# Linear attention of a hybrid block: factor tables by GpSimd beside the statistics, normalised tiles by ScalarE, two constant factors folded into neighbouring operations

## The chip, the cores and the metric

The kernel runs on one core of one Trainium2 chip. The metric is the device time of one execution in microseconds (us), lower is better. All data is fp32; a batch holds 1,024 tokens of 128 channels, and there are 8 batches.

## What is computed

The whole kernel is a chain of a convolutional attention, a whitening, a linear attention, a mixture of experts with GELU, a window attention and a mixture of experts with SiLU. The change touches the linear attention alone. Cut to that:

```python
def _ln_t(v, eps=1e-05):                       # over the 128 channels of a token
    return (v - mean(v)) / sqrt(var(v) + eps)

def _L2_attn_ref(x, kln_weight, kln_bias, vln_weight, vln_bias):
    # 8 heads of 16 channels; k and v are both a layer norm of the head's 16 channels
    q = qkv = x.reshape(B, N, H, hc).transpose(0, 2, 1, 3)
    k = _layernorm(qkv, kln_weight, kln_bias)   # (x - mean) / (std(ddof=1) + 1e-5), then weight and bias
    v = _layernorm(qkv, vln_weight, vln_bias)
    kv = jnp.einsum('bhnd,bhne->bhde', k, v) / N
    out = jnp.einsum('bhnd,bhde->bhne', q, kv)
    return out + x

t = t + _L2_attn_ref(_ln_t(t), ...)
```

## The kernel before, in words

`tokens` is a tensor of 128 partitions x 64 tiles x 128 channels that stays on chip through the program; a batch is 8 of its tiles. `linear_attention` is a block of its own: all engines wait at a barrier before it and after it, so nothing of the stages around it runs beside it. Each engine has its own program, written out by hand, and runs it in that order; semaphores tie the programs together. Most buffers (offset, square, std, scale, z, u, uT, kv) are doubled by the parity of the batch.

- **VectorE** first takes the statistics of all 64 tiles (`TokenNorm.run`, L618 to L650), ending in `norm.mean` and `norm.rstd` (128 x 64). Then it gives `norm_ready` (L770), builds four 128 x 128 tables `factor` (L777 to L781: an outer product of a weight row and a weight column, times a mask of the head blocks), and goes through the batches. One `step(b)` (L839) is: `centre_heads(b+1)` (L791 sum over a head's 16 channels, L792 times 1/16, L793 subtract from the tokens, giving `offset`), `keys(b)` (L811 to L815 on 128 x 64, L816 makes `z`), `variance(b+1)` (L799 sums the squares, L802 times 1/15), `add(b-2)` (L836, twice, adds a result to `tokens`), `combine(b-1)` (L824 to L830, builds the 128 x 128 matrix `kv`). Steps 0, 1 and 7 lack parts of it; steps 2 to 5 stand in a loop, 6 and 7 behind it.
- **ScalarE** per batch: square of `offset(b+1)` (L868), square root (L870) of the variance, and two copies of the transposed tiles, `uT(b)` (L877).
- **GpSimd** makes constants, and then, per batch, the normalised tiles `u` in two operations on 128 x 1024 with broadcast operands (L755, L757); it waits for `norm_ready`, and later for the transposes of two batches before.
- **TensorE** per batch: 8 transposes of `u` (L899, waits for `u` and for `uT` of the batch before), 8 products `z^T z` with a column of ones beside (L903, waits for `z`), 8 column sums (L906), and 8 products of the batch before with `kv` (`give`, L916).
- **SyncE** loads the four small weights at the start (L731, L733).

Of the kernel before, what the change touches and what calls it, by code (L numbers as in the profile page):

```python
# [5 lines left out]
ALU = mybir.AluOpType  # L6
ACT = mybir.ActivationFunctionType
# [662 lines left out]
def linear_attention(nc, ins, ident, tokens):  # L670
# [6 lines left out]
    with ExitStack() as ctx:  # L677
# [11 lines left out]
        var = [t.sbuf(f"lvar{i}", [P, NT * HEADS2]) for i in range(2)]  # L689
# [24 lines left out]
        var_ready = t.sem("lvar_ready")  # L714
        std_ready = t.sem("lstd_ready")
        z_ready = t.sem("z_ready")
        norm_ready = t.sem("lnorm_ready")
        centred = t.sem("lcentred")
# [18 lines left out]
        def _(pool):  # L737
# [11 lines left out]
            def normalise(b, par, first=False):  # L749

                if not first:
                    pool.wait_ge(turn_ready, b - 1)
                at = bass.ds(b * NT, NT)
                over = lambda x: x[:, at].unsqueeze(2).to_broadcast([P, NT, C])
# [12 lines left out]
        def _(dve):  # L767
            norm.run(dve, tokens)

            dve.tensor_copy(term[:, 0:1], norm.rstd[:, 0:1]).then_inc(norm_ready, 1)  # L770
            dve.wait_ge(norm_ready, 1)


            steps = Steps(dve, setup_steps)
            dve.wait_ge(params_loaded, 64)
            dve.wait_ge(blocks_ready, 1)
# [10 lines left out]
            def centre_heads(b, par):  # L787

                centre.round(b)
                batch = tokens[:, bass.ds(b * NT, NT), :].rearrange("p j (h d) -> p (j h) d", h=HEADS2)  # L790
                centre.then(dve.tensor_reduce(head_sum[par][:, :], batch, AX.X, ALU.add))  # L791
                centre.then(dve.tensor_scalar(head_sum[par][:, :], head_sum[par][:, :], 1.0 / HC, None, ALU.mult))  # L792
                dve.tensor_tensor(offset[par][:, :].rearrange("p (g d) -> p g d", d=HC), batch,  # L793
                                  head_sum[par][:, :].unsqueeze(2).to_broadcast([P, NT * HEADS2, HC]),
                                  ALU.subtract).then_inc(offset_ready, 1)

            def variance(b, par):
                dve.wait_ge(square_ready, b + 1)
                dve.tensor_reduce(head_sum[par][:, :], square[par][:, :].rearrange("p (g d) -> p g d", d=HC),  # L799
                                  AX.X, ALU.add).then_inc(squares_summed, 1)  # L800
# [51 lines left out]
            variance(0, 0)  # L852
# [1689 lines left out]
```

## Time and profile before

| | |
|---|---|
| median of 3 runs | 1689.6 us (1680.47 to 1693.16) |
| the profiled execution's own time | 1682.29 us |
| its span, first to last instruction | 1680.4 us |
| mean granted TensorE clock (share of full) | 0.828 |
| busy over the span: PE, DVE, ACT, POOL | 1292.0, 989.6, 519.9, 592.2 us |
| first and last instruction of the linear attention | 297.5 us, 417.7 us |

The span is the time between the first and the last instruction on the chip; the run's time lies 1.9 us above it. PE is TensorE, DVE VectorE, ACT ScalarE, POOL GpSimd. Because of the barriers the linear attention is a stretch of 120 us of its own, and its length adds to the time one for one.

### The profile page before, as it was taken

To read this page: it belongs to the slowest core of one execution; us is meant where nothing else is said; L and a number is where in the kernel's file an instruction comes from. 1 tells how busy PE (TensorE), PEld (TensorE's weight loads), DVE (VectorE), ACT (ScalarE), POOL (GpSimd) and SP (SyncE) were. 2 spreads that over 40 slices of the span, in tenths; PEclk is the share of its full clock that TensorE was granted. 3 is DMA by queue.
4 is the path that set the end of the run, shared out by engine and by line. 5 is a ranking of instruction groups with operands and counts; after the bars stand their busy time and mean duration, and the time that the engine had idled before them with its cause. 6 is when DMAs were issued, how large, how long until landed. Compare 5 with 4: busy or idle time off the path is not lost. (4 is left out here: it accounts for less than half of the span.)

```text
span 1680.4 us, 31908 instructions
## 1 busy us (share of the span) xinstructions
PE 1292.0 (77%) x11786; PEld 1088.7 (65%) x11786; DVE 989.6 (59%) x2376; ACT 519.9 (31%) x1183; POOL 592.2 (35%) x640
## 2 busy tenths in 40 slices
PE   6999987066582999889966775767664999999950
PEld 3555567066572999889953543534453999999950
DVE  3777765898654444455436545643336777788841
ACT  3444420021431545444433221321131233222220
POOL 4000000232145656555025330166103661455554
PEclk9999997589555999999986775666656999999985
DMA  7600000000401333333241200011001332333341
GB/s 278 238 0 1 1 4 0 4 1 0 120 29 61 117 110 115 100 105 111 73 102 41 60 26 1 8 43 42 15 0 55 108 106 85 94 100 105 98 141 50
DMA packets 87890, 115.45 MB, mean 69 GB/s; under 512 B 18695, under 2 KB 70275, under 8 KB 87747
## 3 DMA queue, kind: packets, MB, share of 16 engines
q1 hardware_dynamic: 66786, 62.73, 12.0%
q0 software_dynamic: 20960, 50.76, 9.6%
q8 instruction: 96, 1.57, 0.4%
q14 instruction: 48, 0.39, 0.1%
HBM read 53.01 MB, written 60.42 MB: 68 GB/s over the span
## 5 line engine op out<-in xcount | busy, mean ns | idle before, releaser
L1304 POOL DMA_INDIRECT sorted_rows<-s_normed,s_places x128 | 138.3, 1080 | 222.7 <-POOLq L2404 94.0
L1380 POOL DMA_INDIRECT sx_fetch<-sorted_results,s_places x128 | 132.6, 1036 | 143.1 <-DMA sx_fetch<-sorted_results,s_places 62.1
L1304 POOL DMA_INDIRECT sorted_rows<-g_normed,g_places x128 | 130.2, 1017 | 111.0 <-DMA sorted_rows<-g_normed,g_places 48.7
L1463 PE MATMUL g_bank<-weights,gx_hT 128*128 x1360 | 167.1, 277 | 0.0
L1380 POOL DMA_INDIRECT gx_fetch<-sorted_results,g_places x128 | 125.0, 977 | 114.8 <-DMA gx_fetch<-sorted_results,g_places 64.7
L1463 PEld LDWEIGHTS g_bank<-weights,gx_hT 128*128 128x128 f32 x1360 | 160.1, 193 | 0.2 <-issue 0.2
L1428 PE MATMUL s_bank<-sx_xT_high,sx_w_now 128*128 128x256 f32 (+1 forms) x510 | 151.4, 297 | 1.8 <-DVE sx_hT L1533 1.2
L1430 PE MATMUL s_bank<-sx_xT_high,sx_w_now 128*128 128x256 f32 (+1 forms) x510 | 143.9, 282 | 0.0
L1429 PE MATMUL s_bank<-sx_xT_low,sx_w_now 128*128 128x256 f32 (+1 forms) x510 | 143.8, 282 | 0.0
L1463 PE MATMUL s_bank<-weights,sx_hT 128*128 (+1 forms) x1020 | 130.4, 277 | 7.0 <-issue 4.5
L1488 ACT ACTIVATE gx_hT<-g_bank,gx_b_now 128x256 f32<-128x256 f32 x340 | 133.1, 485 | 3.0 <-PE g_bank L1463 3.0
L1463 PEld LDWEIGHTS s_bank<-weights,sx_hT 128*128 128x128 f32 (+1 forms) x1020 | 120.4, 191 | 12.4 <-issue 12.1
L1428 PE MATMUL g_bank<-gx_xT_high,gx_w_now 128*128 128x256 f32 x340 | 104.6, 308 | 22.9 <-DVE gx_w_now L1516 10.2
L234 PE MATMUL attended<-probs,vs 128*128 128x512 f32 x256 | 120.3, 593 | 0.0
L1481 ACT ACTIVATE sx_xT_high<-s_bank 128x256 fp32r<-128x256 f32 x85 | 32.7, 384 | 241.1 <-PE s_bank L1463 197.2
L339 ACT ACTIVATE probs<-score,nmax 128x1024 f32<-128x1024 f32 x64 | 71.3, 1115 | 113.5 <-DVE nmax L281 113.5
L1542 DVE TENSOR_TENSOR gx_yq<-g_bank,weights 128x256 f32<-128x256 f32 x85 | 36.0, 423 | 119.7 <-PE g_bank L1463 94.7
L281 DVE TENSOR_REDUCE nmax<-score 128x1 f32<-128x1024 f32 x64 | 78.2, 1223 | 46.0 <-PE score L223 46.0
L1429 PE MATMUL g_bank<-gx_xT_low,gx_w_now 128*128 128x256 f32 x340 | 97.6, 287 | 0.0
L1430 PE MATMUL g_bank<-gx_xT_high,gx_w_now 128*128 128x256 f32 x340 | 97.4, 287 | 0.0
L1428 PEld LDWEIGHTS s_bank<-sx_xT_high,sx_w_now 128*128 128x128 f32 (+1 forms) x510 | 90.9, 178 | 2.4 <-issue 2.3
L1481 ACT ACTIVATE gx_xT_high<-g_bank 128x256 fp32r<-128x256 f32 x85 | 32.9, 387 | 188.3 <-PE g_bank L1463 118.5
(404 smaller groups left out, 2920.6 us busy)
## 6 DMA issues: line engine op xcount, KB each, us to landing
sorted_rows<-zeros POOLq DMA_DIRECT2D x29, 512.0 KB, 16.6
gx_xq<-sorted_rows SPq DMA_DIRECT2D x85, 128.0 KB
sorted_results<-gx_yq SPq DMA_DIRECT2D x85, 128.0 KB
sx_xq<-sorted_rows SPq DMA_DIRECT2D x85, 128.0 KB
sorted_results<-sx_yq SPq DMA_DIRECT2D x85, 128.0 KB
feats<-in_x SPq DMA_DIRECT2D x8, 512.0 KB, 4.9
out<-s_normed SPq DMA_DIRECT2D x16, 256.0 KB
g_raw_up<-in_L_ffn_W SPq DMA_DIRECT2D x1, 2048.0 KB, 9.3
```

Of the source, the lines that this page charges most:

```text
L234: done = pe.matmul(out[:, HALF * h:HALF * h + HALF], vs[s % 4][:, :], probs[s % 4][:, HALF * h:HALF * h + HALF], start=(n == 0), stop=(n = ...
L281: dve.tensor_reduce(nmax[s % 4][:, :], score[s % 2][:, :], AX.X, ALU.max, negate=True).then_inc(max_ready, 1)
L339: act.activation(probs[s % 4][:, :], score[s % 2][:, :], ACT.Exp, bias=nmax[s % 4][:, 0:1], accum_out=zsum[s % 4][:, 0:1]).then_inc(exp_do ...
L1304: pool.indirect_dma_start(out=sorted_rows[g], out_offset=bass.IndirectOffsetOnAxis(ap=places[:, at, r:r + 1], axis=0), in_=normed[:, at, : ...
L1380: pool.indirect_dma_start(out=fetch[n % 2][:, i, r, :], out_offset=None, in_=self.sorted_results[g], in_offset=bass.IndirectOffsetOnAxis(a ...
L1428: pe.matmul(out, left[:, part, columns], right[0][:, :], start=True, stop=False)
L1429: pe.matmul(out, left[:, part, columns], right[1][:, :], start=False, stop=False)
L1430: pe.matmul(out, left[:, part + 1, columns], right[0][:, :], start=False, stop=True)
L1463: done = pe.matmul(down[u % 2][:, P * k:P * k + C], hT[u % 2][0:width, i, P * k:P * k + P], self.w_down[0:width, bass.ds(e, 1), i, :].rear ...
L1481: act.activation(xT[u % 2][0][:, :], self.turned[u % 2][:, 0:UNIT], ACT.Copy).then_inc(self.x_high, 1)
L1488: done = act.activation(hT[i][:, k, :], up[i][k // 2][:, k % 2, :], ACT.Gelu, bias=self.b_now[u % 4][:, k:k + 1])
L1542: dve.tensor_tensor(self.yq[u % 4][:, :, :], product, bias, ALU.add).then_inc(self.y_ready, 1)
```

## The change

The four tables `factor` are made on GpSimd right after its constants, as soon as the weights are loaded; VectorE waits for them (`factors_ready`) behind `variance(0)`. `u` is made by ScalarE in 8 instructions of 128 x 128 a batch, `rstd * x + shift`, for which VectorE makes `shift = -mean * rstd` once. The multiplication by 1/16 (L792) goes into the subtraction as a constant of a scalar_tensor_tensor, and that by 1/15 (L802) into the square root's scale.

```diff
-                pool.tensor_tensor(u[par][:, :, :], tokens[:, at, :], over(norm.mean), ALU.subtract).then_inc(centred, 1)
-                pool.wait_ge(centred, b + 1)
-                pool.tensor_tensor(u[par][:, :, :], u[par][:, :, :], over(norm.rstd), ALU.mult).then_inc(u_ready, 1)
...
-            pool.wait_ge(norm_ready, 1)
-            normalise(0, 0, first=True)
-            normalise(1, 1, first=True)
-            with pool.Fori(2, B - 1, 2) as b:
-                normalise(b, 0)
-                normalise(b + 1, 1)
+            factors = Steps(pool, setup_steps)
+            pool.wait_ge(params_loaded, 64)
+            pool.wait_ge(blocks_ready, 1)
+            pairs = ((0, 0, 1.0 / N), (0, 1, 1.0 / N), (1, 0, 1.0 / N), (1, 1, 1.0))
+            for i, (col, row, over) in enumerate(pairs):
+                factors.did(pool.tensor_scalar(factor[i][:, :], rows[:, row, :], column[:, col:col + 1], over,
+                                               ALU.mult, ALU.mult))
+            factors.settle()
+            for i in range(4):
+                factors.did(pool.tensor_tensor(factor[i][:, :], factor[i][:, :], blocks[:, :], ALU.mult))
+            factors.settle()
+            pool.tensor_tensor(factor[3][:, :], factor[3][:, :], ident[:, :], ALU.add).then_inc(factors_ready, 1)
...
-            dve.tensor_copy(term[:, 0:1], norm.rstd[:, 0:1]).then_inc(norm_ready, 1)
-            dve.wait_ge(norm_ready, 1)
-            for i, (col, row, over) in enumerate(((0, 0, 1.0 / N), (0, 1, 1.0 / N), (1, 0, 1.0 / N), (1, 1, 1.0))):
-                steps.then(dve.tensor_scalar(factor[i][:, :], rows[:, row, :], column[:, col:col + 1], over,
-                                             ALU.mult, ALU.mult))
-                steps.then(dve.tensor_tensor(factor[i][:, :], factor[i][:, :], blocks[:, :], ALU.mult))
-            steps.then(dve.tensor_tensor(factor[3][:, :], factor[3][:, :], ident[:, :], ALU.add))
+            dve.scalar_tensor_tensor(out=shift[:, :], in0=norm.mean[:, :], scalar=-1.0, in1=norm.rstd[:, :],
+                                     op0=ALU.mult, op1=ALU.mult).then_inc(norm_ready, 1)
...
                 centre.then(dve.tensor_reduce(head_sum[par][:, :], batch, AX.X, ALU.add))
-                centre.then(dve.tensor_scalar(head_sum[par][:, :], head_sum[par][:, :], 1.0 / HC, None, ALU.mult))
-                dve.tensor_tensor(offset[par][:, :].rearrange("p (g d) -> p g d", d=HC), batch,
-                                  head_sum[par][:, :].unsqueeze(2).to_broadcast([P, NT * HEADS2, HC]),
-                                  ALU.subtract).then_inc(offset_ready, 1)
+                dve.scalar_tensor_tensor(out=offset[par][:, :].rearrange("p (g d) -> p g d", d=HC),
+                                         in0=head_sum[par][:, :].unsqueeze(2).to_broadcast([P, NT * HEADS2, HC]),
+                                         scalar=-1.0 / HC, in1=batch, op0=ALU.mult, op1=ALU.add
+                                         ).then_inc(offset_ready, 1)
...
-                dve.wait_ge(squares_summed, b + 1)
-                dve.tensor_scalar(var[par][:, :], head_sum[par][:, :], 1.0 / (HC - 1), None,
-                                  ALU.mult).then_inc(var_ready, 1)
...
             centre_heads(0, 0)
             variance(0, 0)
+            dve.wait_ge(factors_ready, 1)
...
-                act.wait_ge(var_ready, b + 1)
-                act.activation(std[par][:, :], var[par][:, :], ACT.Sqrt).then_inc(std_ready, 1)
+                act.wait_ge(squares_summed, b + 1)
+                act.activation(std[par][:, :], square_sum[par][:, :], ACT.Sqrt, scale=1.0 / (HC - 1)
+                               ).then_inc(std_ready, 1)
+            def normalise(b, par, first=False):
+                if not first:
+                    act.wait_ge(turn_ready, b - 1)
+                for j in range(NT):
+                    at = bass.ds(b * NT + j, 1)
+                    done = act.activation(u[par][:, j, :], tokens[:, at, :].rearrange("p a c -> p (a c)"), ACT.Identity,
+                                          bias=shift[:, at], scale=norm.rstd[:, at])
+                done.then_inc(u_ready, 1)
...
                 if after:
                     square_of(b + 1, 1 - par)
+                    normalise(b + 1, 1 - par, first=first)
                 act.wait_ge(turn_ready, b + 1)
```

VectorE, between the end of the statistics and the first batches. Before, these rows stood behind the reciprocal that makes `rstd` (the first pair of table rows comes four times in all; `head_sum` is the sum over a head):

```order
L650 RECIPROCAL lnorm_rstd<-lnorm_root 128x64
L770 COPY lterm<-lnorm_rstd 128x1
L778 TENSOR_SCALAR lfactor<-lrows,lcolumn 128x128
L780 TENSOR_TENSOR lfactor<-lfactor,lblocks 128x128
...
L781 TENSOR_TENSOR lfactor<-lfactor,ident 128x128
L791 TENSOR_REDUCE head_sum<-tokens 128x64
L792 TENSOR_SCALAR head_sum<-head_sum 128x64
L793 TENSOR_TENSOR offset<-tokens,head_sum 128x1024
L799 TENSOR_REDUCE head_sum<-square 128x64
L802 TENSOR_SCALAR lvar<-head_sum 128x64
```

Now the same place reads (line numbers of the changed kernel):

```order
L650 RECIPROCAL lnorm_rstd<-lnorm_root 128x64
L766 SCALAR_TENSOR_TENSOR lnorm_shift<-lnorm_mean,lnorm_rstd 128x64
L777 TENSOR_REDUCE head_sum<-tokens 128x64
L778 SCALAR_TENSOR_TENSOR offset<-head_sum,tokens 128x1024
L785 TENSOR_REDUCE lsquare_sum<-square 128x64
```

The nine rows of the tables are gone from VectorE, and so are one row behind each sum over tokens and one behind each sum of squares.

ScalarE, in the first batches. Before (the row on `lnorm_root` is the root of the statistics):

```order
L616 ACTIVATE lnorm_root<-lnorm_eps_var 128x64
L868 ACTIVATE square<-offset 128x1024
L870 ACTIVATE lstd<-lvar 128x64
L868 ACTIVATE square<-offset 128x1024
L870 ACTIVATE lstd<-lvar 128x64
L877 ACTIVATE luT<-lturn 128x512 x2
```

Now:

```order
L616 ACTIVATE lnorm_root<-lnorm_eps_var 128x64
L852 ACTIVATE square<-offset 128x1024
L854 ACTIVATE lstd<-lsquare_sum 128x64
L863 ACTIVATE lu<-tokens,lnorm_shift,lnorm_rstd 128x128 x8
L852 ACTIVATE square<-offset 128x1024
L854 ACTIVATE lstd<-lsquare_sum 128x64
L863 ACTIVATE lu<-tokens,lnorm_shift,lnorm_rstd 128x128 x8
L873 ACTIVATE luT<-lturn 128x512 x2
```

Eight instructions stand between each square root and the copies of the transposed tiles (and, in the first batch, ahead of the second square).

GpSimd, behind its constants. Before, the normalisation stood there, with a loop for batches 2 to 7; now the tables:

```order
L746 AFFINE_SELECT lblocks<-lblocks 128x128
L755 TENSOR_TENSOR lu<-tokens,lnorm_mean 128x1024
L757 TENSOR_TENSOR lu<-lu,lnorm_rstd 128x1024
```

```order
L746 AFFINE_SELECT lblocks<-lblocks 128x128
L754 TENSOR_SCALAR lfactor<-lrows,lcolumn 128x128 x4
L758 TENSOR_TENSOR lfactor<-lfactor,lblocks 128x128 x4
L760 TENSOR_TENSOR lfactor<-lfactor,ident 128x128
```

Sixteen large operations of GpSimd, all behind the statistics, have given way to nine small ones that wait only for the weights.

## Rows read from the trace of the kernel before

**Rows 1.** Stretches: us; PE, PEld, DVE, ACT, POOL busy (count); clock, DMA, GB/s.
```profile
351.80:362.90 11.10, 7.42 (x45) 7.19 (x46) 10.72 (x20) 2.28 (x4) 4.83 (x2) 0.75 0.00 0
395.10:404.40 9.30, 7.49 (x65) 7.06 (x64) 8.92 (x20) 2.28 (x4) 0.00 (x0) 1.00 0.00 0
351.80:404.40 52.60, 37.69 (x280) 35.93 (x280) 50.48 (x92) 11.43 (x20) 18.32 (x8) 0.90 0.00 0
```

**Rows 2.** Timeline where VectorE builds the tables: start us, us, engine, line, operation.
```profile
317.13 0.15 DVE L770 COPY lterm<-lnorm_rstd 128x1 f32<-128x1 f32 x1
...
317.37 1.99 POOL L755 TENSOR_TENSOR lu<-tokens,lnorm_mean 128x1024 f32<-128x1024 f32 x1 [18.65 <-DVE lterm L770]
317.64 1.86 DVE L780 TENSOR_TENSOR lfactor<-lfactor,lblocks 128x128 f32<-128x128 f32 x1
...
329.84 1.22 DVE L791 TENSOR_REDUCE head_sum<-tokens 128x64 f32<-128x1024 f32 x1
```

**Rows 3.** Timeline of step 2, VectorE and GpSimd.
```profile
355.11 1.90 POOL L755 TENSOR_TENSOR lu<-tokens,lnorm_mean 128x1024 f32 x1 [4.32 <-PE lturn L899]
355.54 1.55 DVE L815 TENSOR_TENSOR lscale<-lscale,lnorm_rstd 128x64 f32<-128x64 f32 x1
...
357.17 2.93 POOL L757 TENSOR_TENSOR lu<-lu,lnorm_rstd 128x1024 f32<-128x1024 f32 x1 [0.16 <-POOL lu L755]
...
359.51 0.64 DVE L802 TENSOR_SCALAR lvar<-head_sum 128x64 f32<-128x64 f32 x1
```

**Rows 4.** Groups of instructions, 297 to 418 us: busy us, mean ns, idle before.
```profile
L815 DVE TENSOR_TENSOR lscale<-lscale,lnorm_rstd 128x64 f32<-128x64 f32 x8 | 5.6, 697 | 0.3
...
L826 DVE SCALAR_TENSOR_TENSOR kv<-lfactor,lsums,kv 128x128 f32<-128x128 f32 x8 | 4.6, 578 | 0.3
...
L802 DVE TENSOR_SCALAR lvar<-head_sum 128x64 f32<-128x64 f32 x8 | 4.1, 515 | 0.3
```

**Rows 5.** Timeline of step 6, with no GpSimd work beside it, VectorE.
```profile
395.11 1.21 DVE L791 TENSOR_REDUCE head_sum<-tokens 128x64 f32<-128x1024 f32 x1
...
396.36 0.20 DVE L792 TENSOR_SCALAR head_sum<-head_sum 128x64 f32<-128x64 f32 x1
...
396.58 1.23 DVE L793 TENSOR_TENSOR offset<-tokens,head_sum 128x1024 f32<-128x1024 f32 x1
...
400.20 1.21 DVE L799 TENSOR_REDUCE head_sum<-square 128x64 f32<-128x1024 f32 x1
...
401.44 0.20 DVE L802 TENSOR_SCALAR lvar<-head_sum 128x64 f32<-128x64 f32 x1
401.55 1.28 DVE L836 TENSOR_TENSOR tokens<-tokens,lresult 128x512 f32<-128x512 f32 x2
...
403.13 0.35 DVE L826 SCALAR_TENSOR_TENSOR kv<-lfactor,lsums,kv 128x128 f32<-128x128 f32 x1
...
404.38 0.22 DVE L811 TENSOR_TENSOR lscale<-lstd,lnorm_rstd 128x64 f32<-128x64 f32 x1
```

**Rows 6.** ScalarE's operations, by line: duration ns min/median/max, first and last start.
```profile
L868 ACT ACTIVATE square<-offset x8: 1056/1056/1058, 332.6 to 397.8; 128x1024 f32<-128x1024 f32 x8
...
L877 ACT ACTIVATE luT<-lturn x16: 578/588/597, 341.8 to 408.0; 128x512 f32<-128x512 f32 x16
```

**Rows 7.** Timeline of a later stage: eight of L1147 in a row.
```profile
428.66 3.19 ACT L1147 ACTIVATE g_normed<-tokens,gr_norm_shift,gr_norm_rstd 128x128 f32<-128x128 f32 x8 [0.87 <-DVE gr_norm_shift L1034]
```

**Rows 8.** The weights' last load: its issue, and us to landing in the DMA view.
```profile
298.80 0.43 SPq L733 DMA_DIRECT2D lrows<-in_L_attn_vln_bias  x1
...
lrows<-in_L_attn_vln_bias SPq DMA_DIRECT2D x1, 64.0 KB, 4.2
```

**Rows 9.** GpSimd's nearest small operation, by line, whole program.
```profile
L746 POOL TENSOR_SCALAR_AFFINE_SELECT lblocks<-lblocks 128x128 f32<-128x128 f32 x1 | 0.3, 337 | 0.1
```

**Rows 10.** Timeline: first products of the stage, and its last row.
```profile
340.26 3.71 PE L903 MATMUL gram<-z 128*128 128x129 f32 x16 [16.84 <-DVE z L816]
...
416.40 1.28 DVE L836 TENSOR_TENSOR tokens<-tokens,lresult 128x512 f32<-128x512 f32 x2 [2.21 <-PE lresult L916]
```

More of the change, by code:

```diff
@@ L688, in linear_attention @@
         norm = TokenNorm(t, "l")
-        var = [t.sbuf(f"lvar{i}", [P, NT * HEADS2]) for i in range(2)]
+        shift = t.sbuf("lnorm_shift", [P, TT])
+        square_sum = [t.sbuf(f"lsquare_sum{i}", [P, NT * HEADS2]) for i in range(2)]
         std = [t.sbuf(f"lstd{i}", [P, NT * HEADS2]) for i in range(2)]
@@ L713, in linear_attention @@
         square_ready = t.sem("square_ready")
-        var_ready = t.sem("lvar_ready")
         std_ready = t.sem("lstd_ready")
         z_ready = t.sem("z_ready")
+        factors_ready = t.sem("lfactors_ready")
         norm_ready = t.sem("lnorm_ready")
-        centred = t.sem("lcentred")
         u_ready = t.sem("lu_ready")
@@ L747, in _ @@
                                pattern=[[HC, HEADS2], [0, HC]], channel_multiplier=-1).then_inc(blocks_ready, 1)
[L749 to L754, printed above, removed]
-                pool.tensor_tensor(u[par][:, :, :], tokens[:, at, :], over(norm.mean), ALU.subtract).then_inc(centred, 1)
-                pool.wait_ge(centred, b + 1)
-                pool.tensor_tensor(u[par][:, :, :], u[par][:, :, :], over(norm.rstd), ALU.mult).then_inc(u_ready, 1)
-            pool.wait_ge(norm_ready, 1)
-            normalise(0, 0, first=True)
-            normalise(1, 1, first=True)
-            with pool.Fori(2, B - 1, 2) as b:
-                normalise(b, 0)
-                normalise(b + 1, 1)
+            factors = Steps(pool, setup_steps)
[10 more added lines that the diff above has]
+            pool.tensor_tensor(factor[3][:, :], factor[3][:, :], ident[:, :], ALU.add).then_inc(factors_ready, 1)
         @block.vector
@@ L791, in centre_heads @@
                 centre.then(dve.tensor_reduce(head_sum[par][:, :], batch, AX.X, ALU.add))
-                centre.then(dve.tensor_scalar(head_sum[par][:, :], head_sum[par][:, :], 1.0 / HC, None, ALU.mult))
-                dve.tensor_tensor(offset[par][:, :].rearrange("p (g d) -> p g d", d=HC), batch,
-                                  head_sum[par][:, :].unsqueeze(2).to_broadcast([P, NT * HEADS2, HC]),
-                                  ALU.subtract).then_inc(offset_ready, 1)
+                dve.scalar_tensor_tensor(out=offset[par][:, :].rearrange("p (g d) -> p g d", d=HC),
+                                         in0=head_sum[par][:, :].unsqueeze(2).to_broadcast([P, NT * HEADS2, HC]),
+                                         scalar=-1.0 / HC, in1=batch, op0=ALU.mult, op1=ALU.add
+                                         ).then_inc(offset_ready, 1)
             def variance(b, par):
                 dve.wait_ge(square_ready, b + 1)
-                dve.tensor_reduce(head_sum[par][:, :], square[par][:, :].rearrange("p (g d) -> p g d", d=HC),
+                dve.tensor_reduce(square_sum[par][:, :], square[par][:, :].rearrange("p (g d) -> p g d", d=HC),
                                   AX.X, ALU.add).then_inc(squares_summed, 1)
-                dve.wait_ge(squares_summed, b + 1)
-                dve.tensor_scalar(var[par][:, :], head_sum[par][:, :], 1.0 / (HC - 1), None,
-                                  ALU.mult).then_inc(var_ready, 1)
             def keys(b, par):
@@ L868, in square_of, with batch @@
                 act.activation(square[par][:, :], offset[par][:, :], ACT.Square).then_inc(square_ready, 1)
-                act.wait_ge(var_ready, b + 1)
-                act.activation(std[par][:, :], var[par][:, :], ACT.Sqrt).then_inc(std_ready, 1)
-            def batch(b, par, after=True):
+                act.wait_ge(squares_summed, b + 1)
[9 more added lines that the diff above has]
+                done.then_inc(u_ready, 1)
+            def batch(b, par, after=True, first=False):
                 if after:
                     square_of(b + 1, 1 - par)
+                    normalise(b + 1, 1 - par, first=first)
                 act.wait_ge(turn_ready, b + 1)
@@ L880, in _ @@
             norm.root_of(act)
+            act.wait_ge(norm_ready, 1)
             square_of(0, 0)
-            batch(0, 0)
+            normalise(0, 0, first=True)
+            batch(0, 0, first=True)
             batch(1, 1)
```

3 lines of the change are left out of this document (removed).

## The prediction

> **What bounds the kernel now.** The stage that changes stands between two barriers, so only its own length counts: it runs from 297.5 us to the end of its last row, 416.40 + 1.28 = 417.7 us [rows 10]. The view of busy time by stretch says which engine sets it: over the five steps from 351.8 to 404.4 us VectorE is busy for 50.5 of 52.6 us, TensorE for 37.7, ScalarE for 11.4, GpSimd for 18.3 [rows 1]. VectorE is the bound, and what counts is its queue. Then the timeline, read for operations that take longer than they should. Step 6, where GpSimd has nothing left to do, goes from 395.11 to 404.38, 9.27 us [rows 5]; the four steps ahead of it share the other 52.6 - 9.3 = 43.3 us, 10.8 each [rows 1, 5], with the same instructions. The difference is in small operations beside GpSimd: L815, on 128 x 64 elements, takes 1.55 us and ends at 357.09, where GpSimd's L755 (355.11 to 357.01) has just ended; GpSimd's next one takes 2.93 us instead of 1.90, and L802 starts under it and ends (360.15) as it does (360.10) [rows 3]. The tables at the start show it strongest: L780, on 128 x 128 elements, takes 1.86 us beside L755, more than L793's 1.23 on eight times as many [rows 2, 5]. And all of the tables lie on the path: from 317.13 us to 329.84 us VectorE does nothing for the batches [rows 2].
>
> **The change, part by part.**
>
> *The tables leave VectorE.* Before, `norm_ready` is given by the copy at 317.13 and the first sum over tokens starts at 329.84 [rows 2]. Now one scalar_tensor_tensor on 128 x 64 stands between, of a size with L811's 0.22 us [rows 5]; the sum does not depend on it and starts about 0.15 us after it does: at 317.3. Gain: 329.84 - 317.3 = **12.5 us**. The cover is GpSimd: the last load is issued at 298.80 and lands 4.2 us later, 303.0 [rows 8]. Nine operations on 128 x 128 follow. Their nearest row from below is 0.34 us (one input, same size) [rows 9], from above 1.90 us (two inputs, eight times the elements) [rows 3]. At 0.34 they end at 306.1, at 1.90 at 320.1; I take 0.35 to 0.4, being the same size. VectorE asks for them behind `variance(0)`, at about 322 us (next part), so even the upper bound is hidden; beyond it each us is lost one for one. They now run beside the statistics; should each hold VectorE up for its own length, that costs 9 x 0.35 = 3.2 us, which I keep for the range.
>
> *Two multiplications go.* L792 to L793 is 0.22 us from start to start, L802 to L836 0.11 [rows 5], and both come once per batch: 8 x 0.22 + 8 x 0.11 = **2.6 us**. The subtraction becomes a scalar_tensor_tensor; the trace has that form only on small tiles (L826, 0.35 us undisturbed on 128 x 128 [rows 5]), where the instruction's fixed part weighs most. On 128 x 1024 I take 1.23 us as L793 [rows 5]; 0.1 more on each of eight would cost 0.8. The constant in the square root costs nothing.
>
> *GpSimd's sixteen operations go.* What they did to VectorE stands in the mean durations: L815 0.697 us against 0.23 undisturbed, L826 0.578 against 0.35, L802 0.515 against 0.20 [rows 4, 5]; times eight, 3.7 + 1.8 + 2.5 = **8.0 us**. Cross-check: four steps at 10.8 instead of 9.27 are 6.2 us, the rest lies in step 1. The Trainium skill (SBUF — State Buffer, "Practical consequences" under the ports) says that a VectorE instruction with two SBUF inputs, or in a two-port mode, and a GpSimd one that reads SBUF exclude each other for a whole instruction, and that tensor_reduce never contends. By that rule the whole 8.0 us comes back; if the stretches had another cause, such as the loop, none of it would. The trace bears the rule out: L799 keeps 1.21 us, L815 does not.
>
> *ScalarE takes the normalisation.* Eight of the same form take 3.19 us in a row [rows 7]. Its other four (square, root, two copies) are 2.28 us per step [rows 1], of which the square is 1.06 and the copies, overlapping, the most of the rest [rows 6]. What matters is its cycle: square root, normalise, copies of `uT`, next square, VectorE's sum of squares: 2.28 + 3.19 + 1.21 = 6.7 [rows 1, 5, 7], with handoffs about 7.1 us. VectorE's step is 9.27 - 0.22 - 0.11 = 8.94. ScalarE has 1.8 us of room per step, and one normalising instruction could cost (8.94 - 7.1 + 3.19)/8 = 0.63 us instead of 0.40 before it bounds. In the loop each gets its addresses from registers; VectorE's do too there and keep their durations, so I take 0.40.
>
> The first batches have less room. Walk: sum at 317.3, offset done 319.8, square 320.9, sum of squares until 322.1, step 0 begins at 322.1. It has neither `add` nor `combine`: 401.55 - 395.11 - 0.33 = 6.1 us [rows 5], so step 1 begins at 328.2. In it ScalarE does root (328.5), normalise(1) (331.7), `uT(0)` (332.8), square(2) (333.8); VectorE asks for the square 4.9 us into its step (400.20 - 395.11 - 0.22 [rows 5]), at 333.1. It waits **0.8 us**. What is late next is the square root of batch 2, whose cycle then has the full step of 8.94. No second wait.
>
> *TensorE* keeps its instructions. It is busy 7.5 us per step at full clock [rows 1], so with 8.94 us it has 1.4 us in hand, and results are used one and two steps later. The tail (from 404.38 to 417.7) waits for TensorE's products, whose inputs move with it; it keeps its 13.3 us.
>
> Sum: 12.5 + 2.6 + 8.0 - 0.8 = **22.3 us**. Against the profiled execution's 1682.3 that is 1660.0; that execution is 7.3 us faster than the median of the runs shown (1689.6, spread 12.7). I predict for the median: 1689.6 - 22.3 = **1667 us**, a gain of 1.3%.
>
> The Trainium skill (GPSIMD Engine Reference, "Engine selection") advises VectorE for elementwise work, as GpSimd is about twice as slow with two inputs. By it nine operations at twice VectorE's 0.35 us [rows 5] are an estimated 6.3 us, ending at 309.3 instead of 306.5: the rule speaks against the move where GpSimd is waited for, and changes nothing in the sum here. No row before shows GpSimd on these shapes.
>
> **The rivals.**
>
> *Half the gain.* The stretches inside the steps stay (contention is not their cause, or ScalarE's many small instructions make a new wait of a us per step). Gain 22.3 - 8.0 = 14.3: 1675 us. For it: step 2 to 5 stand in a loop and step 6 does not, so loop and contention coincide there. Against: both ends of the stretches match GpSimd's ends within 0.1 us [rows 3], and L780 at 317.64 is stretched outside any loop [rows 2]. Chance 0.14.
>
> *ScalarE becomes the bound.* Above 0.63 us per normalising instruction. At 1.0 us its cycle is 3.9 + 8 = 11.9 us, 3.0 over VectorE's, seven times: 21 us, nearly all of the gain: 1688. It would take two and a half times the pace of [rows 7]. Chance 0.04.
>
> *TensorE becomes the bound, and the kernel slower.* The granted clock is 0.75 in step 2, 0.90 over the five steps, 1.00 in step 6, and half, 1.2 GHz, at the stage's first products, which take 3.71 us for sixteen after an idle time of 17 us [rows 1, 10]. At 1.2 GHz throughout a batch takes 2 x 7.5 = 15 us; eight from 327 us (340.26 less 13) end at 447, 29 later than now: 1719. It costs something from a mean clock of 7.5/8.94 = 0.84 downwards (TensorE's share at full clock), and eats the gain at 7.5 x 8/(417.7 - 327) = 0.66. Against: 0.90 was granted at a duty of 7.5 in 10.5 us, and the duty now rises to 7.5 in 8.94. Chance 0.05. A clock between 0.75 and 0.84 costs up to 1 us per step and is in the range.
>
> *Tables late.* Over 2.1 us each, more than eight times the elements take. Chance 0.02.
>
> **The numbers.** Forecast 0.73, half 0.14, the others 0.11, something unlooked for 0.02. Range: below, no stall, `shift` for nothing and the low end of the runs' spread give 1655; above, the half gain with 3 to 5 us of contention or clock gives 1680. What one can tell from no change here is about 1%, 17 us; the forecast is 5 us beyond it, and the half gain and some of the forecast's spread fall inside. Faster 0.70, same 0.25, slower 0.05.
>
> **What would show it.** In the profile of the changed kernel: first sum over tokens at about 317.3; nine table rows on GpSimd ending before 310, with VectorE's statistics rows unchanged; L794 to L799 (before L811 to L816) undisturbed; steps of 8.9 us; one wait for a square of about 0.8 us in step 1; eight normalising rows in 3.2 us; last row of the stage at 395. It is wrong if ScalarE's rows in the loop are spaced by over 0.6 us, if VectorE waits for `square` or for TensorE in every step, or if the tables are waited for.

## The result, and the profile after

| | before | changed |
|---|---|---|
| median of 4 runs | 1691.4 us (1680.5 to 1693.6) | 1662.4 us (1659.9 to 1667.8) |
| profiled execution | 1682.3 us | 1660.95 us |
| span of it | 1680.4 us | 1659.0 us |

The ratio is 0.9876, with a 95% interval of 0.9832 to 0.9920: faster by 1.24%, a small gain, but the interval ends below 1. The forecast was 1667 us in a range of 1655 to 1680, with 0.70 on faster.

Runs of one kernel differ by several us, up to 13 us in the kernel before, so the study reads the stage alone: from the issue of its first load to the end of its last addition to `tokens`, both in the trace. It is 417.68 - 297.48 = 120.2 us before (its end in [rows 10]) and 392.04 + 1.28 - 295.77 = 97.55 us after, 22.65 us less; the two profiled executions differ by 21.3 us in all.

The timeline of the changed kernel, the last load's issue by SyncE (SPq) and VectorE, GpSimd and ScalarE between the loads and the second batch (start us, us, engine, line, operation, idle before and its releaser):

```profile
297.09 0.43 SPq L733 DMA_DIRECT2D lrows<-in_L_attn_vln_bias  x1
300.40 1.43 POOL L754 TENSOR_SCALAR lfactor<-lrows,lcolumn 128x128 f32<-128x128 f32 x4 [3.38 <-DMA lrows<-in_L_attn_vln_bias]
300.67 3.88 DVE L621 BATCH_NORM_STATS2 lnorm_bn<-tokens  x16 [0.40 <-issue]
301.92 1.69 POOL L758 TENSOR_TENSOR lfactor<-lfactor,lblocks 128x128 f32<-128x128 f32 x4
303.69 0.45 POOL L760 TENSOR_TENSOR lfactor<-lfactor,ident 128x128 f32<-128x128 f32 x1
...
315.44 0.22 DVE L766 SCALAR_TENSOR_TENSOR lnorm_shift<-lnorm_mean,lnorm_rstd 128x64 f32<-128x64 f32 x1
315.59 1.21 DVE L777 TENSOR_REDUCE head_sum<-tokens 128x64 f32<-128x1024 f32 x1
316.83 1.22 DVE L778 SCALAR_TENSOR_TENSOR offset<-head_sum,tokens 128x1024 f32<-128x1024 f32 x1
...
320.66 3.17 ACT L863 ACTIVATE lu<-tokens,lnorm_shift,lnorm_rstd 128x128 f32<-128x128 f32 x8
```

It answers to [rows 2, 8]. The tables are done at 304.1 us, 16 us ahead of step 0, which asks for them at 320.4, and VectorE's statistics take 3.88 us for sixteen beside them, against 3.86 us in rounds with GpSimd idle. The sum over tokens follows `shift` by 0.15 us. The offset, now a scalar_tensor_tensor, still takes 1.22 us, as in [rows 5].

Two stretches of the same timeline, the wait in step 1 and a step of the loop, VectorE:

```profile
331.76 1.22 DVE L785 TENSOR_REDUCE lsquare_sum<-square 128x64 f32<-128x1024 f32 x1 [0.46 <-ACT square L852]
...
361.21 1.21 DVE L777 TENSOR_REDUCE head_sum<-tokens 128x64 f32 x1
362.46 1.23 DVE L778 SCALAR_TENSOR_TENSOR offset<-head_sum,tokens 128x1024 f32<-128x1024 f32 x1
...
364.67 0.22 DVE L798 TENSOR_TENSOR lscale<-lscale,lnorm_rstd 128x64 f32<-128x64 f32 x1
364.93 1.22 DVE L799 TENSOR_TENSOR z<-offset,lscale 128x1024 f32<-128x1024 f32 x1
366.07 1.21 DVE L785 TENSOR_REDUCE lsquare_sum<-square 128x64 f32<-128x1024 f32 x1
367.20 1.27 DVE L819 TENSOR_TENSOR tokens<-tokens,lresult 128x512 f32 x2
...
370.02 1.21 DVE L777 TENSOR_REDUCE head_sum<-tokens 128x64 f32<-128x1024 f32 x1
```

A step is 370.02 - 361.21 = 8.81 us; the four steps of the loop take 8.8 to 9.0, from 334.55 to 370.02, where the kernel before took 43.3 us for them. L798 and L809, which answer to L815 and L826 in [rows 3, 4], are back at their bare length, in the loop as well. The groups of the changed kernel (busy us, mean ns, idle before):

```profile
L809 DVE SCALAR_TENSOR_TENSOR kv<-lfactor,lsums,kv 128x128 f32<-128x128 f32 x8 | 2.8, 352 | 0.3
...
L798 DVE TENSOR_TENSOR lscale<-lscale,lnorm_rstd 128x64 f32<-128x64 f32 x8 | 1.8, 225 | 0.3
```

TensorE costs something at the end. Here are two stretches of the changed kernel in the columns of [rows 1] (clock third from the end), then TensorE's slow products and VectorE's addition that waits behind them:

```profile
335.00:370.00 35.00, 28.87 (x230) 27.24 (x228) 33.64 (x64) 22.36 (x51) 0.00 (x0) 0.95 0.00 1
374.00:382.00 8.00, 6.98 (x48) 6.98 (x48) 7.11 (x15) 4.30 (x11) 0.00 (x0) 0.79 0.00 0
```
```profile
377.57 2.92 PE L904 MATMUL gram<-z,lones 128*128 128x128 f32 x16
...
382.31 1.28 DVE L819 TENSOR_TENSOR tokens<-tokens,lresult 128x512 f32<-128x512 f32 x2 [0.93 <-PE lresult L914]
```

The stage in three pieces, from the trace:

| us | before | changed | difference | forecast |
|---|---|---|---|---|
| first load to first sum over tokens | 32.36 | 19.82 | -12.54 | -12.5 |
| from there to the keys of step 7 | 74.54 | 63.24 | -11.30 | -9.8 |
| from there to the end | 13.30 | 14.49 | +1.19 | 0 |
| stage | 120.20 | 97.55 | -22.65 | -22.3 |

### The profile page after: what moved, and what is told of

The parts are those of the page before. It is cut to its first block and busy times, and to the rows that moved or that the text cites. A ratio compares the mean times of both kernels' runs of the same rounds, so it can differ in the third digit from the quotient of the medians.

```text
span 1659.0 us, 31967 instructions
## 1 busy us (share of the span) xinstructions
PE 1281.8 (77%) x11786; PEld 1084.3 (65%) x11786; DVE 966.3 (58%) x2351; ACT 545.0 (33%) x1247; POOL 563.6 (34%) x633
## 3 DMA queue, kind: packets, MB, share of 16 engines
q1 hardware_dynamic: 66786, 62.73, 12.2%
## 5 line engine op out<-in xcount | busy, mean ns | idle before, releaser
L1378 POOL DMA_INDIRECT sx_fetch<-sorted_results,s_places x128 | 136.0, 1062 | 149.1 <-DMA sx_fetch<-sorted_results,s_places 60.7
```

The costliest lines, as they stand in the source:

```text
L1378: pool.indirect_dma_start(out=fetch[n % 2][:, i, r, :], out_offset=None, in_=self.sorted_results[g], in_offset=bass.IndirectOffsetOnAxis(a ...
```

## The experiments

Ten kernels were run, in three groups. Where a ratio is given it is to the kernel before, in the same group of runs. e4, e5, e6, e8, e9 and e10 were run once each, so for them only the stage in the trace is read. Two of its three pieces say how well that repeats: the first took 19.80 to 19.82 us in all nine kernels that build the tables on GpSimd, and the last 13.30 to 13.31 us or, where TensorE's clock is low at its start, 14.49 us (changed, e1, e9); only in e6 is it another, 16.06. An operation is called held when it takes longer than its bare length, its shortest time, because it waits for GpSimd; the hold is the difference.

### The tables back on VectorE (e1)

```diff
-            factors = Steps(pool, setup_steps)
...
+            dve.wait_ge(norm_ready, 1)
+            steps = Steps(dve, setup_steps)
...
+                steps.then(dve.tensor_scalar(factor[i][:, :], rows[:, row, :], column[:, col:col + 1], over,
+                                             ALU.mult, ALU.mult))
+                steps.then(dve.tensor_tensor(factor[i][:, :], factor[i][:, :], blocks[:, :], ALU.mult))
+            steps.then(dve.tensor_tensor(factor[3][:, :], factor[3][:, :], ident[:, :], ALU.add))
```

> The change, but with the four tables built by VectorE again, where they stood before; GpSimd makes only its constants and has nothing to do beside VectorE. Stage length is counted from the first load's issue to the end of the last addition: 120.2 us in the kernel before, 97.6 in the changed one. Theory (the 12.5 us of the tables were mostly waits for GpSimd's large operations, L780 1.86 us): nine operations at about 0.3 us each, stage 97.6 + 2.9 = 100.5 us, table rows of 0.29 us. Rival (the tables cost what they cost, wherever GpSimd is): stage 97.6 + 12.5 = 110 us.

Stage 396.32 - 295.69 = 100.6 us, ratio 0.9899 (0.9835 to 0.9964). The timeline of this run at the tables:

```profile
315.60 0.29 DVE L762 TENSOR_SCALAR lfactor<-lrows,lcolumn 128x128 f32<-128x128 f32 x1
315.92 0.29 DVE L764 TENSOR_TENSOR lfactor<-lfactor,lblocks 128x128 f32<-128x128 f32 x1
...
318.19 0.29 DVE L765 TENSOR_TENSOR lfactor<-lfactor,ident 128x128 f32<-128x128 f32 x1
```

All nine take 0.29 us, 2.9 us from the first to the sum over tokens behind them. The theory holds and the rival falls: of the 12.5 us only a quarter was the tables' own work; the rest was GpSimd's normalisation running beside them.

### GpSimd normalises, the rest changed (e2)

GpSimd's part of the kernel before stands again, behind the tables; ScalarE's is taken out.

```diff
+            pool.wait_ge(norm_ready, 1)
+            normalise(0, 0, first=True)
+            normalise(1, 1, first=True)
...
-                    normalise(b + 1, 1 - par, first=first)
```

> The change, but u is normalised by GpSimd in two operations of 128 x 1024 per batch as before, and not by ScalarE; the tables stay on GpSimd ahead of it and the two constants stay folded. Theory (contention between GpSimd and VectorE made the 8 us in the steps): the steps with GpSimd work take about 10.2 to 10.5 us instead of 8.9, and the first four GpSimd operations (7.6 us), which before ran beside the tables, now run beside batches 0 and 1 and hold VectorE there for 0 to 4 us: stage 105.5 to 110 us. Rival (the steps became shorter for another reason, such as the two operations fewer): stage 97 to 99 us.

Stage 408.40 - 298.63 = 109.8 us, ratio 0.9924 (0.9877 to 0.9970), at the upper end of the expected 105.5 to 110. Its timeline shows where the gain of the moved tables went:

```profile
318.61 1.90 POOL L769 TENSOR_TENSOR lu<-tokens,lnorm_mean 128x1024 f32<-128x1024 f32 x1 [11.69 <-DVE lnorm_shift L784]
319.69 1.89 DVE L796 SCALAR_TENSOR_TENSOR offset<-head_sum,tokens 128x1024 f32<-128x1024 f32 x1
320.58 2.76 POOL L771 TENSOR_TENSOR lu<-lu,lnorm_rstd 128x1024 f32<-128x1024 f32 x1
...
326.29 1.92 DVE L812 TENSOR_TENSOR lscale<-lstd,lnorm_rstd 128x64 f32<-128x64 f32 x1
328.09 1.89 POOL L769 TENSOR_TENSOR lu<-tokens,lnorm_mean 128x1024 f32 x1
328.24 1.79 DVE L814 TENSOR_SCALAR lscale<-lscale 128x64 f32<-128x64 f32 x1
```

The same GpSimd operations now hold the offset and the scales of the first batches instead of the tables. There are six of them (batches 0 to 2), here as beside the tables of the kernel before, not the four that the expectation counts. The piece up to the first sum is 12.5 us shorter than in e3 below (19.81 for 32.35), the piece behind it 6.5 us longer (76.66 for 70.13).

### The two folded constants alone (e3)

```diff
-                centre.then(dve.tensor_scalar(head_sum[par][:, :], head_sum[par][:, :], 1.0 / HC, None, ALU.mult))
...
+                dve.scalar_tensor_tensor(out=offset[par][:, :].rearrange("p (g d) -> p g d", d=HC),
...
-                dve.tensor_scalar(var[par][:, :], head_sum[par][:, :], 1.0 / (HC - 1), None,
-                                  ALU.mult).then_inc(var_ready, 1)
...
+                act.activation(std[par][:, :], var[par][:, :], ACT.Sqrt, scale=1.0 / (HC - 1)).then_inc(std_ready, 1)
```

> The kernel before with the two constants folded and nothing else. Theory (prediction's step): 8 x 0.22 + 8 x 0.11 = 2.6 us less, stage 117.6 us. Second possibility within the contention theory: L802 was where VectorE was held, for 2.5 us in sum, and the row behind it has only one input in SBUF and is not held, so that goes too: stage 115 us. Rival (the hold moves to another row): stage 118 to 120 us.

Stage 413.16 - 297.37 = 115.8 us, 4.4 less, ratio 0.9957 (0.9925 to 0.9988). That lies between the two expected values. Holds moved as well as vanished: in the groups of this run L812 is held less than L815 was in [rows 4] (0.697), L823 more than L826 was (0.578), and L826, whose bare length is 0.29 us, is held as well:

```profile
L823 DVE SCALAR_TENSOR_TENSOR kv<-lfactor,lsums,kv 128x128 f32<-128x128 f32 x8 | 6.0, 751 | 0.3
...
L812 DVE TENSOR_TENSOR lscale<-lscale,lnorm_rstd 128x64 f32<-128x64 f32 x8 | 4.6, 576 | 0.3
...
L826 DVE TENSOR_TENSOR kv<-kv,lterm 128x128 f32<-128x128 f32 x8 | 3.7, 467 | 0.3
```

The two folds are worth 3.6 us where nothing is held (8 x 0.45, worked out under the two multiplications below), and L802 takes its hold of 2.5 us with it; of that, about 1.7 us came back on other rows. So the rival's mechanism, the hold that moves, is there too, in part.

With these three runs there is a small table of the stage, all with the constants folded:

| us | GpSimd normalises | ScalarE normalises | difference |
|---|---|---|---|
| tables on VectorE | 115.8 (e3) | 100.6 (e1) | 15.2 |
| tables on GpSimd | 109.8 (e2) | 97.55 (changed) | 12.2 |
| difference | 6.0 | 3.1 | |

The normalisation's move is worth 12 to 15 us, the tables' 3 to 6, and their gains overlap. Both kernels in which ScalarE normalises have the last piece of 14.49 us, the other two 13.30, so without that clock the normalisation's share would be 1.2 us more.

### Unused GpSimd work beside the changed kernel (e4, e8, e9, e10, e5)

All five add two GpSimd operations per batch, on tiles nobody reads, at the places of the old normalisation; what differs is their form. e4:

```diff
+                if not first:
+                    pool.wait_ge(turn_ready, b - 1)
+                for k in range(2):
+                    pool.tensor_tensor(idle[k][:, :], idle[2][:, :], idle[3][:, :], ALU.mult).then_inc(besides, 1)
+                pool.wait_ge(besides, 2 * b + 2)
```

> The changed kernel, with sixteen additional GpSimd operations of 128 x 1024 with two inputs, on tiles of their own that nobody uses, at the places where the normalisation stood before (two per batch, behind the same waits). Theory (contention): VectorE's small operations are stretched again, L798, L809 and those beside, steps of 10.2 to 10.5 us, stage 105.5 to 110 us, as with GpSimd normalising. Rival (the dependence on u mattered, not the port): stage 97.6 us.

Stage 416.74 - 298.80 = 117.9 us. The rival falls: no batch needs this work, and the stage is 20.4 us longer. But it is 8 us more than expected. Two things plainly differ from the old normalisation: no wait stands between the two, and both operands are full, which makes them longer: 2.35 us instead of 1.90.

e8 has the wait (the second reads what the first wrote):

```diff
+                pool.tensor_tensor(idle[par][:, :], idle[2][:, :], idle[3][:, :], ALU.mult).then_inc(besides, 1)
+                pool.wait_ge(besides, 2 * b + 1)
+                pool.tensor_tensor(idle[par][:, :], idle[par][:, :], idle[3][:, :], ALU.mult).then_inc(besides, 1)
```

> As the run with reading GpSimd operations beside (stage 117.9 us, where the two of a batch stood back to back and z was held for 2.0 us on average), but the second reads what the first wrote and waits for it, as the normalisation did. Theory (the wait leaves a gap of 0.16 us in which a waiting VectorE operation gets in, and then GpSimd waits for it): z back to 1.23 us, GpSimd's second operation at 2.9 us in some batches, stage 108 to 111 us, as with GpSimd normalising (109.8). Rival (the gap makes no difference): 117 to 119 us.

Stage 416.36 - 297.02 = 119.3 us: the time is the rival's. Its timeline shows the race for `z`:

```profile
350.20 2.34 POOL L773 TENSOR_TENSOR idle<-idle 128x1024 f32<-128x1024 f32 x1 [3.63 <-PE lturn L919]
350.44 2.18 DVE L820 TENSOR_TENSOR lscale<-lscale,lnorm_rstd 128x64 f32<-128x64 f32 x1
352.62 2.34 POOL L775 TENSOR_TENSOR idle<-idle 128x1024 f32<-128x1024 f32 x1
352.65 3.38 DVE L821 TENSOR_TENSOR z<-offset,lscale 128x1024 f32<-128x1024 f32 x1
```

GpSimd's second operation starts 0.03 us ahead of `z`, and `z` takes 3.38 us instead of 1.23, in three of the eight batches. The expectation took a gap of 0.16 us between the two from the old normalisation; here it is 352.62 - (350.20 + 2.34) = 0.08 us, too short for `z`.

e9 has the wait and the old form, with a broadcast column as second operand:

```diff
+                pool.tensor_tensor(idle[par][:, :, :], idle[2][:, :, :], over(norm.mean), ALU.subtract).then_inc(besides, 1)
+                pool.wait_ge(besides, 2 * b + 1)
+                pool.tensor_tensor(idle[par][:, :, :], idle[par][:, :, :], over(norm.rstd), ALU.mult).then_inc(besides, 1)
```

> GpSimd operations nobody uses beside the changed kernel once more, but in exactly the form of the normalisation: the second operand is a broadcast column (1.90 us each; with two full operands they took 2.35), and the second waits for the first. Theory (who gets the port is decided within some hundredths of a us: with this form VectorE's z starts just ahead of GpSimd's second operation, as in the kernel before, and is not held): z at 1.23 us, stage 107 to 111 us. Rival (the form is no matter, the unused operations hold VectorE for longer because ScalarE normalises and GpSimd starts earlier in the step): stage 116 to 120 us.

Stage 405.15 - 297.13 = 108.0 us, within the theory's 107 to 111 and near e2's 109.8 (its last piece has the 1.2 us of TensorE's clock). In its timeline the order is the other way round:

```profile
344.02 1.90 POOL L774 TENSOR_TENSOR idle<-idle,lnorm_mean 128x1024 f32<-128x1024 f32 x1 [3.73 <-PE lturn L920]
344.17 1.83 DVE L821 TENSOR_TENSOR lscale<-lscale,lnorm_rstd 128x64 f32<-128x64 f32 x1
346.03 1.23 DVE L822 TENSOR_TENSOR z<-offset,lscale 128x1024 f32<-128x1024 f32 x1
346.08 2.94 POOL L776 TENSOR_TENSOR idle<-idle,lnorm_rstd 128x1024 f32<-128x1024 f32 x1 [0.16 <-POOL idle L774]
```

`z` starts 0.05 us ahead, keeps its 1.23 us, and it is GpSimd that waits (2.94 us). So a few hundredths of a us decide which of the two pays, and they are those of the gap: in both runs `z` starts 0.11 us after the end of GpSimd's first operation (352.54 in e8, 345.92 in e9), GpSimd's second 0.08 us after it in e8 and 0.16 in e9. All meetings of this kind in the traces agree: in e8 `z` is 0.03 us behind in three batches and held in each; it is 0.04 to 0.05 us ahead in two batches of e9 and e3 each and in three of e2 and of the kernel before, and never held.

Why the gaps differ was not tested. The broadcast operand alone is not the reason, since in e9 the pairs of batches 0 and 1, ahead of the loop, stand 0.07 and 0.08 us apart. What e9, e2 and the kernel before have inside the loop, and e8 lacks, are operands whose place depends on the batch. So e8 and e9 differ in three things, the length, the operand and the gap.

e10 is e9's form without the wait:

```diff
+                for k, table in enumerate((norm.mean, norm.rstd)):
+                    pool.tensor_tensor(idle[k][:, :, :], idle[2][:, :, :], over(table), ALU.mult).then_inc(besides, 1)
```

> As the run before it, but without the wait between the two GpSimd operations of a batch, so that they stand back to back. Theory (without a gap the second keeps the port and z waits for it as well): z held to about 2 us on average, stage 115 to 119 us. Rival (VectorE gets in between the two all the same): stage as with the wait.

Stage 406.54 - 296.80 = 109.7 us, 1.7 more than with the wait, and not the 115 to 119 expected. The mechanism is there:

```profile
345.69 1.90 POOL L773 TENSOR_TENSOR idle<-idle,lnorm_rstd 128x1024 f32<-128x1024 f32 x1
345.85 2.82 DVE L820 TENSOR_TENSOR z<-offset,lscale 128x1024 f32<-128x1024 f32 x1
```

and `z`, held in two batches, averages 1.62 us against 1.23 in e9, 3.2 us over eight batches, but not to the 2 us expected. The rest of the difference is spread over other rows. One of them, in e10 and then in e9:

```profile
L830 DVE SCALAR_TENSOR_TENSOR kv<-lfactor,lsums,kv 128x128 f32<-128x128 f32 x8 | 4.6, 572 | 0.3
```
```profile
L832 DVE SCALAR_TENSOR_TENSOR kv<-lfactor,lsums,kv 128x128 f32<-128x128 f32 x8 | 2.9, 368 | 0.3
```

It costs 1.6 us more; a smaller hold of `kv<-kv,lterm` (0.61 us on average against 0.80) gives 1.5 back. Between the first sum and the last keys e10 is 2.9 us longer (76.62 for 73.71), and its last piece is 1.2 us shorter, because TensorE's clock was not low there. So the missing wait cost about 3 us, and most of e4's and e8's excess came with the other form of the operations. Between e8 and e9 that excess is 12.5 us in the same piece (86.22 for 73.71). `z` alone makes 6.5 of it (three times 2.15 us); the remaining 6 are holds of other rows, behind operations that are each 0.45 us longer. An effect of the length by itself was not measured.

e5 lets GpSimd write only:

```diff
+                pool.tensor_tensor(tiny[:, 0:1], tiny[:, 1:2], tiny[:, 2:3], ALU.mult).then_inc(besides, 1)
+                for k in range(2):
+                    pool.memset(idle[k][:, :], 1.0).then_inc(besides, 1)
```

> As the run with reading GpSimd operations beside the changed kernel (stage 117.9 us), but the sixteen large ones are memsets of 128 x 2048, about 1.9 us each, which write and read nothing (ahead of each pair stands one multiplication of one column, for the wait). Theory A (a VectorE operation with two SBUF inputs is only kept out by a GpSimd operation that reads SBUF): L798, L799, L809, L812, L813 keep their undisturbed 0.23 to 1.23 us, at most the tensor_scalar L796 is held now and then: stage 98 to 100 us. Theory B (any GpSimd operation on SBUF keeps them out): stage 106 to 118 us.

Stage 396.17 - 299.75 = 96.4 us, below even the theory's 98 to 100, because its last piece (13.30 us) lacks the 1.2 us that the changed kernel lost to TensorE's clock. Its groups:

```profile
L773 POOL MEMSET idle<- 128x2048 f32 x16 | 28.4, 1804 | 0.0
...
L820 DVE TENSOR_TENSOR z<-offset,lscale 128x1024 f32<-128x1024 f32 x8 | 9.8, 1225 | 0.3
...
L817 DVE TENSOR_SCALAR lscale<-lscale 128x64 f32<-128x64 f32 x8 | 2.1, 261 | 0.3
L819 DVE TENSOR_TENSOR lscale<-lscale,lnorm_rstd 128x64 f32<-128x64 f32 x8 | 1.8, 225 | 0.3
```

28 us of GpSimd work beside the batches, and no VectorE operation with two inputs is held; only the tensor_scalar L817 grows, from 0.20 to 0.26 us on average (0.64 and 0.28 in two batches, bare in six). So it is GpSimd's reading that keeps the two-input operations out. The tensor_scalars are another matter: beside reading GpSimd operations they are held too (L802 in [rows 3, 4], L814 in e2), and this run shows one held beside a writing one. The Trainium skill says the same (SBUF — State Buffer, "Practical consequences": two SBUF inputs contend with a GpSimd instruction that reads SBUF, not with one that only writes it).

### ScalarE normalises twice (e6)

```diff
+                    act.activation(spare[par][:, j, :], tokens[:, at, :].rearrange("p a c -> p (a c)"), ACT.Identity,
+                                   bias=shift[:, at], scale=norm.rstd[:, at])
```

> The changed kernel, with every tile normalised a second time by ScalarE into a spare tile: sixteen instead of eight instructions per batch, 3.2 us more. Theory (ScalarE's cycle is 2.28 + 3.19 + 1.21 + handoffs = 7.0 us, so there are 1.9 us of room): the cycle becomes 10.2 us and bounds; VectorE waits for square in every step, 1.3 us in the steady ones, about 3 in each of the first three: stage 97.6 + 14 = 111 to 112 us. Rival (ScalarE has more room, or the instructions overlap): stage 97.6 to 104 us.

Stage 408.80 - 298.68 = 110.1 us. The view of waits gives VectorE's (us in total, times, longest), and a steady step shows 0.80 us of it:

```profile
DVE lsquare_sum L786 <- ACT square L853: 12.1, 8, 3.5
```
```profile
359.72 1.22 DVE L786 TENSOR_REDUCE lsquare_sum<-square 128x64 f32<-128x1024 f32 x1 [0.80 <-ACT square L853]
```

ScalarE bounds now: the last three whole steps, from 353.98 to 383.05, take 9.91, 9.47 and 9.69 us, where 10.2 was expected. The mechanism is as forecast, and the stage is 1 to 2 us shorter than expected: an instruction costs 0.385 us from start to start instead of 0.40, 0.24 us per batch of sixteen, and the rest of the half us per step was not separated. So the cycle with eight instructions, put at 7.0 to 7.1 us, is an estimated 9.7 - 8 x 0.385 = 6.6 us.

### Fewer small operations, a version that beats both (e7)

```diff
-                spread = norm.rstd[:, bass.ds(b * NT, NT)].unsqueeze(2).to_broadcast([P, NT, HEADS2])
-                front.then(dve.tensor_tensor(scales, std[par][:, :].rearrange("p (j h) -> p j h", h=HEADS2),
-                                             spread, ALU.mult))
-                front.then(dve.tensor_scalar(scale[par][:, :], scale[par][:, :], HEAD_EPS, None, ALU.add))
-                front.then(dve.reciprocal(scale[par][:, :], scale[par][:, :]))
-                front.then(dve.tensor_tensor(scales, scales, spread, ALU.mult))
+                spread = eps_root[:, bass.ds(b * NT, NT)].unsqueeze(2).to_broadcast([P, NT, HEADS2])
+                front.then(dve.tensor_tensor(scales, std[par][:, :].rearrange("p (j h) -> p j h", h=HEADS2),
+                                             spread, ALU.add))
+                front.then(dve.reciprocal(scale[par][:, :], scale[par][:, :]))
...
+                both = gram[par][:, :].rearrange("p (a c) -> p a c", a=2)[:, :, 0:C]
+                back.then(dve.tensor_tensor(terms[:, :, :], both, pair[:, :, :], ALU.mult))
...
+            act.activation(eps_root[:, :], norm.eps_var[:, :], ACT.Sqrt, scale=HEAD_EPS ** 2).then_inc(eps_ready, 1)
```

> A version meant to beat both kernels, built on the changed one: the head's factor is made as 1 / (std + eps * root) instead of rstd / (std * rstd + eps), with eps * root from one ScalarE operation on the statistics, which takes L796 and L798 (0.23 + 0.26 us) out of every batch; and the two products of gram with tables become one operation on a pair of tables (about 0.19 us less). Theory (VectorE's queue is still the bound, 8.8 us per step, ScalarE's cycle 7.0): 8 x 0.68 = 5.4 us less, of which 0.5 is lost in step 1, where VectorE waits longer for square: stage 92.6 us. Rival (ScalarE or TensorE is already level with VectorE): stage 95 to 97.6 us, with new waits of VectorE.

Stage 388.05 - 295.70 = 92.35 us, 5.2 less than the changed kernel; 1659.0 us median (1654.2 to 1661.6, 6 runs), ratio 0.9832 (0.9782 to 0.9881). Its overlap with the changed kernel's interval leaves the whole time open between the two; the stage settles it in part. Of the 5.2 us, 4.0 lie between the first sum and the last keys (59.25 for 63.24) and come from the shorter steps; 1.2 us are the last piece, 13.30 for 14.49, since TensorE's clock was not low there this time. The expected 92.6 us was met with the help of that: the 4.9 us it counts on take in operations of the last piece too, and what is saved there does not shorten it, for it is 13.30 us in the kernel before as well. A step in its timeline:

```profile
358.49 1.21 DVE L782 TENSOR_REDUCE head_sum<-tokens 128x64 f32 x1
...
361.13 0.55 DVE L801 RECIPROCAL lscale<-lscale 128x64 f32<-128x64 f32 x1
361.71 1.23 DVE L802 TENSOR_TENSOR z<-offset,lscale 128x1024 f32<-128x1024 f32 x1
...
365.25 0.41 DVE L812 TENSOR_TENSOR lterms<-gram,lpair 128x256 f32<-128x256 f32 x1
...
366.62 1.21 DVE L782 TENSOR_REDUCE head_sum<-tokens 128x64 f32<-128x1024 f32 x1
```

8.13 us from sum to sum, 0.68 less, to the hundredth what was expected of a step: in the steps VectorE's queue is still what bounds. The new waits for TensorE's results stand in the last piece alone (0.24 and 0.26 us).

## Why the prediction was right, point by point

- **What bounds.** VectorE's queue, from the first sum over tokens on: right. e7 shows it from the other side (what is taken from the queue comes back), e6 where it ends.
- **The tables, 12.5 us.** Measured 12.54. The size was right, the account too short: the gain was put down to the tables' move alone. e1 and e2 show that the tables' own work is 2.9 us; the other 9.6 us was contention with the normalisation, and would in part have moved to the first batches had that stayed on GpSimd (e2 is 6.0 us shorter than e3, not 12.5). The prediction had seen L780's stretch in [rows 2] and did not carry it into this term.
- **Hidden behind the statistics.** Right: the operations took 0.37 and 0.45 us each (0.35 to 0.4 was forecast; VectorE takes 0.29 in e1, so GpSimd is 1.3 and 1.5 times as long, not twice), ended at 304.1, and held nothing up; the 3.2 us kept for the range were not needed.
- **Two multiplications, 2.6 us.** Mis-sized. The offset starts 1.24 us behind the sum (316.83 - 315.59) instead of 1.47 in [rows 5], 0.23 as forecast. But the addition follows the sum of squares at 367.20 - 366.07 = 1.13 us, where [rows 5] have 401.55 - 400.20 = 1.35: 0.22 instead of 0.11. The multiplication had waited for the sum; what stands there now does not, and starts before the sum has ended. So the term, 2.6 in the forecast, was 8 x 0.45 = 3.6 us. In e3, beside GpSimd and with holds moving, the stage lost 4.4.
- **The stretches, 8.0 us.** Of the three groups of [rows 4] two are back at 225 and 352 ns, and the third is gone: right. e9, e4 and e5 show the cause, with no batch waiting for the work that does it. 2.5 of the 8 us were the hold of L802, a tensor_scalar.
- **ScalarE.** Eight in 3.17 us, no wait in the steady steps, and one in step 1: right in place, 0.46 us instead of 0.8.
- **TensorE and the tail, no cost.** Missed by 1.2 us. The granted clock was 0.95 from 335 to 370 us, but 0.79 from 374 to 382: sixteen products took 2.92 us instead of 1.95, and VectorE, in the short step 7, waited 0.93 us for the results of the batch two before. The rival named this as a price within the range; in e5, e7 and e10 the last piece was 1.2 us shorter, as before the change, in e1 and e9 it was not. Which stretch gets the lower clock changes from kernel to kernel.
- **The sum.** -12.5 - 3.6 - 8.1 + 0.5 + 1.2 = -22.5, measured -22.65; forecast -22.3. The 1.0 us that the folds gave beyond their forecast and the 1.2 us that the tail lost cancelled; that the sum comes within 0.4 us is luck to this extent.
- **The rivals.** Half the gain: refuted by L798 and L809 in the loop, and by e9. ScalarE as the bound: real, but at a doubled load. TensorE as the bound: not here, and seen only as the 1.2 us. Tables late: 16 us away.
- **The base.** Taking the gain off the median gave 1667, taking it off the profiled execution gave 1660; the runs have 1662.4. The six further us between medians (29.0) and stage (22.65) lie within the spread of the kernel before, 13 us among four runs, and no gain of the change can be shown in them.

## What to carry to other kernels

GpSimd operations that read SBUF can cost the vector engine more than they save, when nothing waits for their result: look for small two-input operations and tensor_scalars of VectorE whose lengths vary and that end when a GpSimd operation ends, and add up their mean less their shortest. Then move the large GpSimd operation, not the small ones it holds: here that was worth 12 to 15 us, and moving the held tables alone only 6. GpSimd did no harm beside VectorE's statistics (3.88 us a round for 3.86), and next to none when it only wrote; and ScalarE, with eight small instructions for one large one, was the better place as long as its cycle stayed under VectorE's step.

## What the runs showed of the hardware that was not expected

- Order decides by hundredths: with GpSimd 0.03 us ahead, `z` took 3.38 us (e8); with `z` 0.05 us ahead, it took 1.23 us and GpSimd 2.94 (e9). A wait between two GpSimd operations left a gap of 0.16 us in one kernel's loop (e9) and of 0.08 in another's (e8), and only the longer one let `z` in.
- A GpSimd tensor_tensor on 128 x 1024 takes 1.90 us with a broadcast column as second operand (e9) and 2.35 us with two full ones (e8).
- In the changed kernel VectorE's next instruction starts 1.13 us after the start of a tensor_reduce of 1.21 us when it does not wait for its result (367.20 - 366.07), and 1.24 us when it does (316.83 - 315.59). A fold that takes a dependent operation away can so gain 0.1 us more than the distance behind that operation shows.
